# Cross attention and a gated mixture of projections: G/U slots moved by four places, loads and logits put earlier, ten weight pieces later

## Chip, core and metric

One core of one Trainium2 chip. The time is device time in microseconds (us) of one execution. PE is TensorE, DVE VectorE, ACT ScalarE, POOL GpSimd, SP SyncE, which here only issues DMAs.

## What is computed

64 batches of x (256 tokens x 256 channels), each with 77 context rows of 192 channels, all float32:

```python
def xattn(x, context):                     # 8 heads of 64
    q, k, v = heads(x @ Wq), heads(context @ Wk), heads(context @ Wv)
    return merge(softmax(q k^T / 8) v) @ Wo + bo
def ffn(h):                                # 16 experts
    rw = gating(h)      # softmax over the experts whose logit is positive (the top two if none is)
    q, k, v = [sum_e rw[:, e] * (h @ proj[e]) for proj in (q_proj, k_proj, v_proj)]
    attn = softmax(causal(q k^T / 8)) v
    return sum_e (attn * rw[:, e]) @ o_proj[e]
x = x + xattn(layernorm(x), ctx)
x = x + ffn(layernorm(x))
```

Gating's logits are `normalize(h) @ normalize(sim) - sigmoid(gates)`.

## The kernel before

**Products.** Every float32 operand is split into hi and lo parts (ACT writes hi, DVE subtracts to get lo), and `product` multiplies lo\*hi, hi\*lo and hi\*hi: lines 478, 479 and 480. Any product in the profile is in those lines, told apart by its tiles.

**Three phases, one step.** Phase a is cross attention of batch i+1, phase b the second layernorm, gating and expert projections of batch i, phase c the attention and output of batch i-1 (its last product, `c_y`, is of i-2). `step(i)` runs for i from -2 to 65, and each engine has its own hand-written order of the same step; semaphores join them. A step has an early half (slots E0 to E3, between scores of a and projections `b_qkv` 6 to 15) and a late half (M1, transpose XT, M2, `c_qk`, `b_qkv` 0, M3, `b_qkv` 1 and 2, `c_s`, the product Y with `uo`, `c_pT`, `b_qkv` 3, `c_pv`, `b_qkv` 4, L1, `b_qkv` 5, L2). I count position in a step from XT (line 537).

**G and U.** The context side is folded into the weights: for three batches (a group gm) 25 jobs make keys k0 to k3, values v0 to v3, G (k times Wq, g0 to g7) and U (v times Wo, u0 to u7), from the transposed context `ct`. The table `JOBS` puts them into the slots of three steps (i%3 = 0, 1, 2; I call these step 0, 1, 2). g0 to g7 and u0 to u7 go through one of two `draft` buffers (f%2) to DRAM (`store_g`, `store_u`), and come back per batch (`load_g` into `gq`, `load_u` into `uo`). `j_g(gm, f)` waits for k(f//2) to be taken out of PSUM, `j_u` for v(f//2). The jobs and phase a share three PSUM banks in the ring `A_ORDER`.

**Order of the loads.** SP issues in order and waits in order: behind a store that waits for DVE, every load waits too. `load_u(n)` needs all U of the group stored and Y of batch n-1 done; `load_x(n)` needs the sum xb of batch n-1 (POOL) and its layernorm.

**Gating chain.** `b_top` on DVE (logits z, line 1244, and top 8), `b_route_1` and `b_route_2` on POOL, `b_exp` on ACT, `b_wsum` on DVE, `b_rw` on POOL (line 1529). `b_first` on ACT (line 936) then scales `b_qkv` 0 and 1 by rw and frees their bank; PE needs that bank for `b_qkv` 3. `b_exp` stands on ACT behind `c_exp`, which needs `c_s` of DVE (line 1295).

**Opening.** Ahead of step -2 the group 0 is made in one go (`OPENING`), and the weights come in 16 pieces through three staging areas; pieces 6 to 13 are the expert projections (three DMAs each), 14 and 15 o_proj. `SPLIT_AFTER` puts pieces 6 to 10 into the opening, 11 to 15 are split in step -1.

Of the kernel before, what the change touches and what calls it, by code (L numbers as in the profile page):

```python
# [34 lines left out]
def xattn_moe_kernel(nc, x, ctx_in, Wq, Wk, Wv, Wo, bo, sim_matrix, gates, q_proj, k_proj, v_proj, o_proj, out, rw_dram):  # L35
# [67 lines left out]
    def job(i, slot):  # L103

        if slot not in JOBS[i % 3]:
            return None
        kind, f = JOBS[i % 3][slot]
        gm = i // 3 + (2 if kind == "ct" or i % 3 == 2 and kind != "u" else 1)
        return (gm, kind, f) if 1 <= gm < GROUPS else None
# [6 lines left out]
    with es:  # L116
# [219 lines left out]

        def loads_before(piece):
            return sum(len(PIECES[k][0]) for k in range(piece % SLOTS, piece + 1, SLOTS))
# [9 lines left out]
        def _(sp):  # L348
# [62 lines left out]
            def load_weights(pieces):  # L411
                for k in pieces:
                    if k >= SLOTS:
                        sp.wait_ge(wt_ready, k - SLOTS + 1)
                    for view, src in PIECES[k][0]:
                        sp.dma_start(view(stage[k % SLOTS]), src).then_inc(wt_in[k % SLOTS], 16)
# [7 lines left out]
            def step(i):  # L424
# [7 lines left out]

                if i % 3 == 2 and i // 3 + 3 < GROUPS:
# [4 lines left out]
                if i == -1:  # L438
                    load_weights((14,))
                if on(i + 2) and i + 2 > 0:  # L440
                    load_g(i + 2)
                if i == -1:
                    load_weights((15,))
# [6 lines left out]
                turn("E3")  # L450
                turn("M1")
                turn("M2")
# [6 lines left out]
            for hc, pieces in enumerate(((6,), (7, 8), (9,), (10, 11))):  # L459
                store_g(0, 2 * hc)  # L460
                store_g(0, 2 * hc + 1)
                load_weights(pieces)
            load_g(0)
            for hc, pieces in enumerate(((12,), (13,), (), ())):
                store_u(0, 2 * hc)
                store_u(0, 2 * hc + 1)
                load_weights(pieces)
# [7 lines left out]
        def _(pe):  # L475
# [257 lines left out]
            for k, (kind, f) in enumerate(OPENING):  # L733
                if k >= A_BANKS:
                    taken(0, *OPENING[k - A_BANKS])
                if kind == "ct":
                    j_ct(0)
                    query_weights()
                elif kind == "k":
                    j_k(0, f)  # L740
                elif kind == "v":
# [85 lines left out]
        def _(act):  # L827
# [6 lines left out]
            def split_weights(k):  # L834
                hi = PIECES[k][1]
                act.wait_ge(wt_in[k % SLOTS], 16 * loads_before(k))
                nc.scalar.activation(hi, stage[k % SLOTS][:, 0:hi.shape[1]], copy).then_inc(wt_hi, 1)
# [170 lines left out]
            for kind, f in OPENING:  # L1008
                if kind == "ct":
                    j_ct(0)  # L1010
                    query_weights()
                    ln1_b(0)
                elif kind == "k":
                    j_k(0, f)
                elif kind == "v":
# [8 lines left out]
            def step(i):  # L1024
# [22 lines left out]
                if i == -1:  # L1047
                    split_weights(11)
# [4 lines left out]
                if i == -1:  # L1053
                    split_weights(12)
                do(now, ln2_b)
                turn("E1")
                turn("E2")
# [4 lines left out]
                if i == -1:  # L1062
                    split_weights(13)
# [12 lines left out]
                if i == -1:  # L1076
                    split_weights(15)
# [10 lines left out]
                do(before, c_mix, 3)  # L1088
                turn("L2")

# [5 lines left out]
        def _(dve):  # L1096
# [11 lines left out]
            def split_weights(k):  # L1108
                dve.wait_ge(wt_hi, k + 1 if k < CC else k + 1 - CC)
                for lo, hi, rows, cols in PIECES[k][2]:  # L1110
                    last = V.tensor_tensor(lo, stage[k % SLOTS][rows, cols], hi.bitcast(F32), ALU.subtract)
# [212 lines left out]
            def step(i):  # L1324
# [23 lines left out]
                if i == -1:  # L1348
                    split_weights(11)
# [13 lines left out]
                do(now, b_norm, 2)  # L1363
                do(before, b_qkv, 11)
                if i == -1:
                    split_weights(12)
                turn("E1")
                do(earlier, c_y)
# [6 lines left out]
                if i == -1:  # L1375
                    split_weights(13)
# [13 lines left out]
                if i == -1:  # L1390
                    split_weights(15)
# [14 lines left out]
                do(now, b_qkv, 5)  # L1406
# [210 lines left out]
```

## Time and profile before

| | us |
|---|---|
| median of 3 runs | 2858.8 |
| lowest, highest | 2854.28, 2860.21 |
| the profiled execution | 2861.3 |
| its span | 2859.5 |
| PE busy in it | 2559.7 |
| DVE, ACT, POOL busy | 2158.7, 1581.5, 1105.5 |
| PE idle before Y (line 478, `uo`) | 83.3 in 21 waits |
| PE idle before `b_qkv` 3 | 73.0 in 43 waits |

Busy time of PE counts pipelined matmuls and is not PE at its peak. "<- issue" names no engine: the last semaphore came from something that the profile can't name, such as two DMAs counted by one semaphore.

### The profile page before, as it was taken

What the parts mean: (1) busy time and instruction counts of PE and PEld (TensorE: products, weight loads), DVE (VectorE), ACT (ScalarE), POOL (GpSimd) and SP (SyncE); (2) the same over time, 40 slices, a digit from 0 to 9 for tenths busy, and PEclk for the clock granted to TensorE, in tenths of its full rate; (3) what the DMA queues carried; (4) which work ended last, traced back from release to release, by engine and by line L of the source; (5) the groups of instructions that cost most, each with busy time, mean ns of one, the idle gap of its engine ahead of it and who ended that gap; (6) DMA issues with size and microseconds to landing.
All of it is one profiled execution on the core that took longest, in us unless ns stands there. A gap on an engine that the chain in (4) does not pass through costs nothing.

```text
span 2859.5 us, 54177 instructions
## 1 busy us (share of the span) xinstructions
PE 2559.7 (90%) x17308; PEld 2482.2 (87%) x17308; DVE 2158.7 (75%) x6107; ACT 1581.5 (55%) x5110; POOL 1105.5 (39%) x1739
## 2 busy tenths in 40 slices
PE   4599898999999898999899898999989899999987
PEld 3588898989889898989899898989889899989886
DVE  5477787877787787877777787877778787878774
ACT  4565565655555565555555565555555565556542
POOL 0134344434334344434334344434434434434442
PEclk6699999999999999999999999999999999999998
DMA  7555554454554554454555554454555455465531
GB/s 197 170 155 167 159 172 139 154 179 144 169 160 156 155 165 144 149 178 143 165 152 163 162 164 142 150 179 144 171 168 161 142 170 155 147 183 149 161 107 41
DMA packets 299938, 445.78 MB, mean 156 GB/s; under 512 B 36856, under 2 KB 210872, under 8 KB 291464
## 3 DMA queue, kind: packets, MB, share of 16 engines
q1 hardware_dynamic: 230024, 374.15, 41.2%
q10 hardware_dynamic: 69632, 68.17, 10.1%
q8 instruction: 140, 2.29, 0.4%
q14 instruction: 142, 1.16, 0.1%
HBM read 257.91 MB, written 184.35 MB: 155 GB/s over the span
## 4 chain that ended last, share of the span: by engine, by line
PE 62%; issue 11%; ACT 9%; POOL 7%; DVE 6%; ACTq 3%; DMA 2%; SPq 0%; POOLq 0%; DVEq 0%
PE bank_b L478 9%; PE bank_b L479 9%; PE bank_b L480 9%; PE bank_c L478 4%; PE bank_c L479 4%; PE bank_c L480 4%; PE bank_a L478 4%; PE bank_a L479 4%; PE bank_a L480 4%; ACTq L996 3%; POOL probs L1553 2%; PE bank_a L611 2%; PE bank_a L578 1%; DVE acc L1275 1%; DMA u_dram<-draft 1%
## 5 line engine op out<-in xcount | busy, mean ns | idle before, releaser
L478 PE MATMUL bank_b<-wqkv_hi,x2T_lo 128*128 128x384 f32 (+1 forms) x2048 | 732.1, 357 | 73.3 <-ACT acc L936 73.0
L1275 DVE SCALAR_TENSOR_TENSOR acc<-bank_b,rw,acc 128x192 f32<-128x192 f32 x1792 | 653.6, 410 | 93.5 <-PE bank_b L480 89.6
L479 PE MATMUL bank_b<-wqkv_lo,x2T_hi 128*128 128x384 f32 (+1 forms) x2048 | 698.0, 341 | 0.0
L480 PE MATMUL bank_b<-wqkv_hi,x2T_hi 128*128 128x384 f32 (+1 forms) x2048 | 695.0, 339 | 0.0
L1558 POOL TENSOR_TENSOR mixs_lo<-mix,mixs_hi 128x512 fp32r<-128x512 f32 x256 | 381.0, 1520 | 428.9 <-ACT mixs_hi L1005 428.9
L478 PEld LDWEIGHTS bank_b<-wqkv_hi,x2T_lo 128*128 128x128 f32 x2048 | 391.3, 191 | 85.2 <-ACT acc L936 83.4
L906 ACT ACTIVATE probs<-bank_a,s_max 128x77 f32<-128x77 f32 x1024 | 318.5, 327 | 259.3 <-DVE s_max L1208 259.0
L479 PEld LDWEIGHTS bank_b<-wqkv_lo,x2T_hi 128*128 128x128 f32 x2048 | 391.3, 191 | 0.0
L480 PEld LDWEIGHTS bank_b<-wqkv_hi,x2T_hi 128*128 128x128 f32 x2048 | 389.1, 190 | 0.0
L1553 POOL TENSOR_TENSOR probs<-probs,p_sum 128x616 f32<-128x616 f32 x128 | 156.6, 1223 | 393.7 <-DVE p_sum L1215 393.7
L1316 DVE TENSOR_TENSOR mix<-rw_all,late_tiles 128x512 f32<-128x512 f32 x256 | 281.1, 1138 | 24.5 <-ACT late_tiles L1001 24.5
L478 PE MATMUL bank_c<-wo_hi,mixs_lo 128*128 128x256 f32 x1024 | 287.6, 281 | 3.7 <-POOL mixs_lo L1558 3.7
L480 PE MATMUL bank_c<-wo_hi,mixs_hi 128*128 128x256 f32 x1024 | 286.8, 280 | 0.0
L479 PE MATMUL bank_c<-wo_lo,mixs_hi 128*128 128x256 f32 x1024 | 286.6, 280 | 0.0
L478 PE MATMUL bank_a<-uo,pT_lo 128*128 128x256 f32 (+1 forms) x640 | 203.1, 317 | 83.4 <-issue 83.3
L1005 ACT ACTIVATE mixs_hi<-mix 128x512 fp32r<-128x512 f32 x256 | 159.8, 632 | 158.8 <-DVE mix L1316 158.8
L1538 POOL TENSOR_TENSOR mix<-acc 128x192 f32<-128x192 f32 x128 | 76.3, 596 | 374.1 <-DVE acc L1275 373.0
L478 PEld LDWEIGHTS bank_a<-uo,pT_lo 128*128 128x128 f32 (+1 forms) x640 | 142.4, 223 | 87.4 <-issue 87.0
L906 ACT ACTIVATION_READ_ACCUMULATOR probs<-bank_a,s_max 128x1 f32 x1024 | 210.9, 206 | 0.0
L1181 DVE TENSOR_TENSOR both<-bank_a,only 64x231 fp32r<-64x231 f32 x352 | 138.9, 395 | 84.1 <-ACT both L865 81.7
L479 PE MATMUL bank_a<-uo,pT_hi 128*128 128x256 f32 (+1 forms) x640 | 199.4, 312 | 0.0
L480 PE MATMUL bank_a<-uo,pT_hi 128*128 128x256 f32 (+1 forms) x640 | 198.1, 309 | 0.0
(206 smaller groups left out, 6472.6 us busy)
## 6 DMA issues: line engine op xcount, KB each, us to landing
g_dram<-draft SPq DMA_DIRECT2D x176, 462.0 KB
gq<-g_dram SPq DMA_DIRECT2D x64, 1232.0 KB, 5.7
uo<-u_dram SPq DMA_DIRECT2D x64, 1024.0 KB
rw_all<-rw_dram ACTq DMA_DIRECT2D x128, 512.0 KB, 7.1
u_dram<-draft SPq DMA_DIRECT2D x176, 308.0 KB
xt<-in_x_dram SPq DMA_DIRECT2D x64, 256.0 KB, 4.2
out_dram<-mix SPq DMA_DIRECT2D x64, 256.0 KB, 6.3
u_dram<-draft SPq DMA_DIRECT2D x88, 156.0 KB
```

Source lines behind the costliest of these rows:

```text
L478: nc.tensor.matmul(dst, lhs[1], rhs[0], start=start, stop=False)
L479: nc.tensor.matmul(dst, lhs[0], rhs[1], start=False, stop=False)
L480: return nc.tensor.matmul(dst, lhs[0], rhs[0], start=False, stop=stop)
L906: last = nc.scalar.activation(probs[:, t, h * NC:(h + 1) * NC], bank_a(f"S{j}")[:, k * NC:(k + 1) * NC], ACT.Exp, bias=s_max[:, j, k:k + 1 ...
L996: nc.scalar.dma_start(rw_all[k * D:(k + 1) * D, :, :], rw_dram[:, :].rearrange("(a k) t -> k a t", k=2)[k].partition_broadcast(D)).then_in ...
L1005: nc.scalar.activation(mixs[0][:, 2 * j:2 * j + 2, :], mix[:, 2 * j:2 * j + 2, :], copy).then_inc(mix_hi, 1)
L1181: last = V.tensor_tensor(both[rows, k, e, cols], src[rows, cols], only.bitcast(F32)[rows, k, e, cols], ALU.subtract)
L1275: V.scalar_tensor_tensor(acc[:, t, k, :], src, rw[:, t, e:e + 1], acc[:, t, k, :], ALU.mult, ALU.add).then_inc(b_evac, 1)
L1316: V.tensor_tensor(mix[:, 2 * j:2 * j + 2, :], rw_all[:, 2 * j:2 * j + 2, :], aT2[:, :].unsqueeze(1).to_broadcast([P, 2, T]), ALU.mult).the ...
L1538: G.tensor_tensor(qkv[:, t, :], acc[:, t, 0, :], acc[:, t, 1, :], ALU.add).then_inc(qkv_ready, 1)
L1553: G.tensor_tensor(part, part, p_sum[:, half, 1, :, :].unsqueeze(3).to_broadcast([P, NT, HB, NC]), ALU.mult).then_inc(p_ready, 1)
L1558: G.tensor_tensor(mixs[1][:, 2 * j:2 * j + 2, :], mix[:, 2 * j:2 * j + 2, :], mixs[0].bitcast(F32)[:, 2 * j:2 * j + 2, :], ALU.subtract).t ...
```

## The change

1. `JOBS`: the jobs stand one to three slots earlier than before, k2 alone stays in L1 (g0 to g3 and k0 to k3 are now all in step 2, g4 opens step 0, and u6, u7 end step 1 instead of opening step 2). U of a new group is loaded at the head of step 2.
2. SP: `load_x(i+3)` at the end of step i instead of `load_x(i+2)` near its start; POOL: `a_xb(i+2)` at the end of step i instead of `a_xb(i+1)` between `c_mix` and `power` at its start.
3. DVE: `b_top` ahead of `c_qk`, `b_index` ahead of slot M2.
4. Opening: pieces 6 to 15 are split in steps -1, 0 and 1; `query_weights` runs behind k1; pieces get an explicit staging table.

```diff
-    JOBS = ({"E0": ("g", 3), "E1": ("k", 3), "E2": ("g", 4), "E3": ("g", 5), "M1": ("v", 0), "M2": ("g", 6), "L1": ("g", 7),
-             "L2": ("v", 1)},
-            {"E0": ("u", 0), "E1": ("u", 1), "E2": ("v", 2), "E3": ("u", 2), "M1": ("u", 3), "M2": ("v", 3), "M3": ("u", 4),
-             "L1": ("ct", 0), "L2": ("u", 5)},
-            {"E0": ("u", 6), "E1": ("u", 7), "E2": ("k", 0), "E3": ("k", 1), "M1": ("g", 0), "M2": ("g", 1), "L1": ("k", 2),
-             "L2": ("g", 2)})
+    JOBS = ({"E0": ("g", 4), "E1": ("g", 5), "E2": ("v", 0), "E3": ("g", 6), "M1": ("g", 7), "M2": ("u", 0), "L1": ("v", 1),
+             "L2": ("u", 1)},
+            {"E0": ("v", 2), "E1": ("u", 2), "E2": ("u", 3), "E3": ("v", 3), "M1": ("u", 4), "M2": ("u", 5), "M3": ("ct", 0),
+             "L1": ("u", 6), "L2": ("u", 7)},
+            {"E0": ("k", 0), "E1": ("g", 0), "E2": ("k", 1), "E3": ("g", 1), "M1": ("g", 2), "M2": ("g", 3), "L1": ("k", 2),
+             "L2": ("k", 3)})
...
+        STAGE = (0, 1, 2, 0, 1, 2, 0, 1, 2, 0, 1, 2, 1, 2, 1, 1)
...
-        SPLIT_AFTER = {("k", 1): (W_V,), ("k", 2): (W_O - 1, W_O), ("k", 3): (6,), ("v", 0): (7,), ("v", 1): (8,),
-                       ("u", 0): (9,), ("u", 2): (10,)}
+        SPLIT_AFTER = {("k", 1): (W_V,), ("k", 2): (W_O - 1, W_O)}
...
 # SP, step(i)
+                if i % 3 == 2 and on(i + 1) and i + 1 > 0:
+                    load_u(i + 1)
                 turn("E0")
-                if on(i + 2) and i + 2 > 0:
-                    load_x(i + 2)
...
                 turn("E1")
-                if i % 3 == 2 and on(i + 1) and i + 1 > 0:
-                    load_u(i + 1)
...
                 turn("M2")
-                turn("M3")
                 if i % 3 != 1 and on(i + 2):
                     load_u(i + 2)
+                if on(i + 3) and i + 3 > 0:
+                    load_x(i + 3)
                 turn("L1")
...
 # DVE, step(i)
                 do(nxt, a_xT)
+                do(now, b_top)
                 do(before, c_qk)
+                do(now, b_index)
                 turn("M2")
-                do(now, b_top)
-                do(now, b_index)
                 do(before, c_s)
...
 # POOL, step(i)
                 for j in range(4):
                     do(earlier, c_mix, j)
-                do(ahead, a_xb)
...
                 do(now, b_rw)
+                do(nxt, a_xb)
```

The weight pieces' loads and splits stand in the same way in the steps: 6, 7, 8 are loaded behind g7's store and split at E1, E2, M1 of step -1; 9 and 10 in L1 and L2 of step -1; 11 to 14 in step 0; 15 in step 1 (it was 11 to 15 in step -1).

SP around the head of a step 2, before (from the context loads to the step's U load and the output store; `draft` rows are stores of u6, then u7):

```order
L363 DMA ct<-in_ctx_dram 116x192
L364 DMA ct<-in_ctx_dram 116x64
L363 DMA ct<-in_ctx_dram 115x192
L364 DMA ct<-in_ctx_dram 115x64
L378 DMA u_dram<-draft 77x2x512
L378 DMA u_dram<-draft 39x2x512
L353 DMA xt<-in_x_dram 128x2x256
L388 DMA gq<-g_dram 128x2464
L378 DMA u_dram<-draft 38x2x512
L378 DMA u_dram<-draft 77x2x512
L397 DMA uo<-u_dram 128x4x512
L399 DMA uo<-u_dram 104x512
```

The same place now:

```order
L379 DMA u_dram<-draft 38x2x512
L379 DMA u_dram<-draft 77x2x512
L364 DMA ct<-in_ctx_dram 116x192
L365 DMA ct<-in_ctx_dram 116x64
L364 DMA ct<-in_ctx_dram 115x192
L365 DMA ct<-in_ctx_dram 115x64
L398 DMA uo<-u_dram 128x4x512
L400 DMA uo<-u_dram 104x512
L389 DMA gq<-g_dram 128x2464
```

The U load stands directly behind the context loads, u6 and u7 are stored before them, and x was loaded before this point.

DVE in the late half of a step 2, before (xT\_lo is behind XT, L1286 is `c_qk`, the draft is slot M2's, L1244 to L1257 are `b_top` and `b_index`, L1295 is `c_s`):

```order
L1167 TENSOR_TENSOR xT_lo<-bank_a,xT_hi 128x512
L1286 TENSOR_TENSOR mixs_hi<-bank_c,q_rows 64x256
L1286 TENSOR_TENSOR mixs_hi<-bank_c,mixs_hi 64x256
L1196 TENSOR_TENSOR draft<-bank_a,draft 128x2x3x77
L1244 SCALAR_TENSOR_TENSOR z<-bank_b,rn,sig 128x16 x2
L1249 MAX top<-z 128x8 x2
L1255 MAX_INDEX idx<-top,z 128x8 x2
L1257 CAST idxf<-idx 128x16
L1295 ISA mix,m<-bank_c,causal 128x128
```

And now:

```order
L1183 TENSOR_TENSOR xT_lo<-bank_a,xT_hi 128x512
L1260 SCALAR_TENSOR_TENSOR z<-bank_b,rn,sig 128x16 x2
L1265 MAX top<-z 128x8 x2
L1302 TENSOR_TENSOR mixs_hi<-bank_c,q_rows 64x256
L1302 TENSOR_TENSOR mixs_hi<-bank_c,mixs_hi 64x256
L1271 MAX_INDEX idx<-top,z 128x8 x2
L1273 CAST idxf<-idx 128x16
L1212 TENSOR_TENSOR draft<-bank_a,draft 128x2x3x77
L1311 ISA mix,m<-bank_c,causal 128x128
```

z and its maximum went ahead of `c_qk`, and the draft behind the index.

PE where step 2 meets step 0, now (the last row of k3 in slot L2, `b_qkv` 6, then g4 in E0, which needs k2 of slot L1):

```order
L561 MATMUL bank_a<-cT_hi,wk_hi 128x232
L482 MATMUL bank_b<-wqkv_hi,x2T_lo 128x384
L483 MATMUL bank_b<-wqkv_lo,x2T_hi 128x384
L484 MATMUL bank_b<-wqkv_hi,x2T_hi 128x384
L482 MATMUL bank_b<-wqkv_hi,x2T_lo 128x384
L483 MATMUL bank_b<-wqkv_lo,x2T_hi 128x384
L484 MATMUL bank_b<-wqkv_hi,x2T_hi 128x384
L582 MATMUL bank_a<-both,wq 128x232
```

Before, L2 held g2 and E0 held g3, which both need k1 of slot E3; k2 was first needed by g4 in E2 of step 0.

## Rows read from the trace of the kernel before

**Rows 1.** The page: span, busy time and share, granted clock in 40 slices

```profile
span 2859.5 us, 54177 instructions
PE 2559.7 (90%) x17308; PEld 2482.2 (87%) x17308; DVE 2158.7 (75%) x6107; ACT 1581.5 (55%) x5110; POOL 1105.5 (39%) x1739
PEclk6699999999999999999999999999999999999998
```

**Rows 2.** Waits of PE, whole span: total us, times, longest us

```profile
PE bank_a L478 <- issue: 83.3, 21, 4.9
PE bank_b L478 <- ACT acc L936: 73.0, 43, 2.0
PE bank_a L611 <- POOL probs L1553: 43.8, 21, 8.8
PE bank_a L578 <- DVE both L1181: 12.4, 22, 2.9
```

**Rows 3.** Timeline, PE and ACT, late half of step 32: start, us, [idle <-releaser]

```profile
1501.56 0.28 PE L680 MATMUL bank_c<-mixs_hi,q_rows 128*128 128x256 f32 x1
1505.02 0.55 PE L478 MATMUL bank_a<-uo,pT_lo 128*128 128x256 f32 x1 [3.18 <-issue]
1511.37 0.42 PE L478 MATMUL bank_b<-wqkv_hi,x2T_lo 128*128 128x384 f32 x1
1506.26 0.73 ACT L936 ACTIVATE acc<-bank_b,rw 128x192 f32<-128x192 f32 x2 [2.26 <-POOL rw L1529]
```

**Rows 4.** Timeline, SP: u5's store, x load, u7's store, U load

```profile
1472.97 0.64 SPq L378 DMA_DIRECT2D u_dram<-draft  x2
...
1480.66 0.51 SPq L353 DMA_DIRECT2D xt<-in_x_dram  x1
1489.07 0.66 SPq L378 DMA_DIRECT2D u_dram<-draft  x2
1496.54 0.38 SPq L397 DMA_DIRECT2D uo<-u_dram  x1
```

**Rows 5.** Timeline, DVE and POOL, early half of step 32

```profile
1486.17 0.75 DVE L1126 BATCH_NORM_STATS2 stats<-xt 128x6 f32<-128x256 f32 x2 [3.79 <-DMA xt<-in_x_dram]
1487.77 1.22 POOL L1553 TENSOR_TENSOR probs<-probs,p_sum 128x616 f32<-128x616 f32 x1 [5.42 <-DVE p_sum L1215]
```

**Rows 6.** Busy by stretch: length, engines, PEclk, DMA share, GB/s

```profile
1503.70:1510.50 6.80, 5.48 (x26) 5.51 (x27) 1.07 (x5) 1.03 (x5) 1.70 (x6) 0.50 0.35 118
1462.80:1466.20 3.40, 3.40 (x14) 3.40 (x13) 2.08 (x6) 0.85 (x3) 0.00 (x0) 0.50 0.12 44
52.00:82.00 30.00, 8.30 (x30) 6.25 (x29) 7.77 (x13) 6.95 (x16) 0.00 (x0) 0.50 0.65 189
```

**Rows 7.** Timeline, step 30, XT at 1410.66: `b_qkv` 1, then the gating chain

```profile
1413.93 0.34 PE L480 MATMUL bank_b<-wqkv_hi,x2T_hi 128*128 128x400 f32 x1
1415.86 0.37 DVE L1244 SCALAR_TENSOR_TENSOR z<-bank_b,rn,sig 128x16 f32<-128x16 f32 x2
1417.17 0.29 DVE L1295 CUSTOM_DVE_ANT_0 mix<-bank_c,causal 128x128 f32<-128x128 f32 x1
1418.40 0.21 ACT L926 ACTIVATE w<-g 128x32 f32<-128x32 f32 x1
1420.60 0.24 POOL L1529 TENSOR_TENSOR rw<-w,w_sum 128x32 f32<-128x32 f32 x1 [0.50 <-DVE w_sum L1263]
1421.66 0.44 PE L478 MATMUL bank_b<-wqkv_hi,x2T_lo 128*128 128x384 f32 x1 [1.67 <-ACT acc L936]
```

**Rows 8.** Timeline, PE and DVE, step 32 into 33: k2's evacuation and E0

```profile
1517.82 0.27 PE L578 MATMUL bank_a<-both,wq 128*128 128x232 f32 x1
1519.63 0.80 DVE L1181 TENSOR_TENSOR both<-bank_a,only 64x231 fp32r<-64x231 f32 x2 [0.36 <-ACT both L865]
```

**Rows 9.** Timeline, opening, DVE and PE

```profile
81.00 0.69 DVE L1203 TENSOR_TENSOR draft<-bank_a,draft 116x512 fp32r<-116x512 f32 x1 [3.97 <-ACT draft L899]
101.96 2.37 PE L611 MATMUL bank_a<-ident,probs 128*128 128x128 f32 x10 [8.79 <-POOL probs L1553]
```

More of the change, by code:

```diff
@@ L107, in job @@
         kind, f = JOBS[i % 3][slot]
-        gm = i // 3 + (2 if kind == "ct" or i % 3 == 2 and kind != "u" else 1)
+        gm = i // 3 + (2 if kind == "ct" or i % 3 == 2 else 1)
         return (gm, kind, f) if 1 <= gm < GROUPS else None
@@ L335, in xattn_moe_kernel @@
         assert len(PIECES) == W_O2 + 1 and all(piece[1] is None or piece[1].shape[1] <= SP_COLS for piece in PIECES)
+        STAGE = (0, 1, 2, 0, 1, 2, 0, 1, 2, 0, 1, 2, 1, 2, 1, 1)
         def loads_before(piece):
-            return sum(len(PIECES[k][0]) for k in range(piece % SLOTS, piece + 1, SLOTS))
-        SPLIT_AFTER = {("k", 1): (W_V,), ("k", 2): (W_O - 1, W_O), ("k", 3): (6,), ("v", 0): (7,), ("v", 1): (8,),
-                       ("u", 0): (9,), ("u", 2): (10,)}
+            return sum(len(PIECES[k][0]) for k in range(piece + 1) if STAGE[k] == STAGE[piece])
+        SPLIT_AFTER = {("k", 1): (W_V,), ("k", 2): (W_O - 1, W_O)}
         block = es.enter_context(nc.Block())
@@ L413, in load_weights @@
                     if k >= SLOTS:
-                        sp.wait_ge(wt_ready, k - SLOTS + 1)
+                        sp.wait_ge(wt_ready, max(p for p in range(k) if STAGE[p] == STAGE[k]) + 1)
                     for view, src in PIECES[k][0]:
-                        sp.dma_start(view(stage[k % SLOTS]), src).then_inc(wt_in[k % SLOTS], 16)
+                        sp.dma_start(view(stage[STAGE[k]]), src).then_inc(wt_in[STAGE[k]], 16)
             load_weights(range(0, 1))
@@ L450, in step @@
                 turn("E3")
+                weights(-1, 10)
                 turn("M1")
+                weights(-1, 11)
+                weights(0, 14)
                 turn("M2")
-                turn("M3")
                 if i % 3 != 1 and on(i + 2):
                     load_u(i + 2)
+                if on(i + 3) and i + 3 > 0:
+                    load_x(i + 3)
                 turn("L1")
                 turn("L2")
[L459 to L462, printed above, removed]
+            for f in range(H):
+                store_g(0, f)
             load_g(0)
[L464 to L467, printed above, removed]
+            load_weights(range(6, 9))
+            for f in range(H):
+                store_u(0, f)
             load_u(0)
@@ L737, in _ @@
                     j_ct(0)
-                    query_weights()
                 elif kind == "k":
                     j_k(0, f)
+                    if f == 1:
+                        query_weights()
                 elif kind == "v":
@@ L1010, in _ @@
                     j_ct(0)
-                    query_weights()
-                    ln1_b(0)
                 elif kind == "k":
                     j_k(0, f)
+                    if f == 1:
+                        query_weights()
+                        ln1_b(0)
                 elif kind == "v":
@@ L1110, in split_weights @@
                 for lo, hi, rows, cols in PIECES[k][2]:
-                    last = V.tensor_tensor(lo, stage[k % SLOTS][rows, cols], hi.bitcast(F32), ALU.subtract)
+                    last = V.tensor_tensor(lo, stage[STAGE[k]][rows, cols], hi.bitcast(F32), ALU.subtract)
                 last.then_inc(wt_ready, 1)
@@ L1406, in step @@
                 do(now, b_qkv, 5)
+                if i == -1:
+                    split_weights(9)
+                if i == 0:
+                    split_weights(14)
                 turn("L2")
+                if i == -1:
+                    split_weights(10)
             dve.wait_ge(small_in, 48)
@@ L1432, in _ @@
                     j_ct(0)
-                    query_weights()
                 elif kind == "k":
                     j_k(0, f)
+                    if f == 1:
+                        query_weights()
                 elif kind == "v":
```

63 lines of the change are left out of this document (40 added, 23 removed).

## The prediction

> **What bounds the kernel.** The page comes first: PE is busy 90% of the span, DVE 75%, and nothing else is near [rows 1]. So PE sets the time, and what can be won lies in three places: its idle time, the stretches at the lower clock, and the two ends. The matmuls themselves stay as they are. Next the waits of PE [rows 2]: 83.3 us before Y, 21 times and thus once in three steps; 73.0 us before `b_qkv` 3, 43 times, so in two steps of three; 43.8 us before the transposes of probs, 21 times. Third the timeline around one wait of each kind [rows 3, 5, 7], to see who is late and what PE loses in all. A loss counts here from where PE would have gone on, since the wait before Y has a longer shadow than its idle time: the granted clock was 0.50 over the stretch that holds it [rows 6], that is 1.2 GHz, where nearly every slice of the page has nine tenths or more of 2.4 [rows 1]. Groups of three steps repeat 21 times, so the sum is made for one group and multiplied. It is made against the profiled execution's 2861.3 us, 2.5 above the median of 2858.8.
>
> **U of a new group (step 2).** Before, u7 is stored at 1489.07 and the load is issued at 1496.54, when that store has landed; the first matmul that needs it starts at 1505.02 [rows 3, 4]. Store to load is 7.5 us and load to use 8.1 us (1505.02 less 1496.97, where its second DMA goes out). Now u7 is in slot L2 of step 1, where u5 was: stored at 1472.97 [rows 4]. The load can go at about 1472.97 + 7.5 = 1480.5 and is in at 1488.6 to 1489, some 13 us before PE asks at 1501.84 (the end of 1501.56 + 0.28, rows 3). Even if the steps shrink by 3 us it is hidden. The SP queue stands still for those 7.5 us behind u7; what queues behind it is the load of G, which waits for this step's last scores anyway, and g0's store.
> What that gives: Y and `c_pT` occupied PE from 1505.02 to 1511.37, mostly at half clock [rows 3, 6]. At full clock throughout the same 33 instructions take less, between 3.2 (half) and 6.35 us; I take 3.9, since the last part ran at full clock already. PE would be at `b_qkv` 3 at 1505.7 (it starts Y right behind `c_s`, at 1501.73), where the next wait is late: ACT frees the bank with the instruction of 1506.26 + 0.73 = 1507.0 [rows 3]. So the removed wait gives 1511.37 - 1507.05 = 4.3 us, and a gating wait of 1.3 us comes to light in step 2.
> The Trainium skill, page "TensorE: Matmul & The Clock Gate", section "HAM oscillation — how this bites in real kernels", says that a long DMA wait inside a matmul loop sends the array back to the slow clock, so that each next piece starts cold. By that rule, the trace agrees: the clock of the first row of rows 6. It would leave short waits free of charge. The second row of rows 6 speaks against that here: 0.50 right behind a gating wait of 1.72 us.
>
> **x earlier.** In step 2 the load of x stands behind the context loads and u6's store and goes out at 1480.66 [rows 4]; DVE waits 3.79 us for it, and p_sum, probs and the transposes follow [rows 5]. In the other steps x is in time. Now it is issued behind xb at the end of the step before, more than 20 us ahead, so this wait and PE's 43.8 us go. Of these 13.3 are the opening's (8.79 of them in one wait [rows 9]); 30.5 / 18 = 1.7 us per group. Next late there is PE itself. POOL's xb, 1.3 us, moves from a place where POOL waits for DVE later anyway to one where it has just written rw and is idle: nothing.
>
> **Logits ahead.** In step 30 z starts at 1415.86, 5.2 us behind XT, DVE having done `c_qk` and M2 first; z needs only `b_qkv` 1, which PE ends at 1413.93 + 0.34 = 1414.27 [rows 7]. So z can start 1.5 us sooner. What then sets rw? Not POOL's part but the two things that join it: `b_exp` at 1418.40 on ACT, which stands behind `c_exp` and so behind `c_s` at 1417.17, and on DVE `c_p` ahead of `b_wsum` [rows 7]. `c_s` hardly moves: `c_qk` now ends 0.4 us later (z and the maximum are ahead of it), PE's `c_s` follows by as much, and DVE gets there at about 1417.0. From there: `c_p` done 1419.1, `b_wsum` 1419.5, rw 1419.9, bank free 1420.7 instead of 1421.6. Gain 0.9 us, with PE's own 0.4 us at `c_s` already inside, since the bank is still last. Bounds: 0 (if M2's draft waits for the store of E3, which now uses the same draft buffer, and holds `c_s` back) and 1.67, the whole wait. I take 0.9 in steps 0 and 2. In step 1 slot M3 (now `ct`, 0.6 us on DVE) lies between `c_p` and `b_wsum`, so 0.3. Together 2.1 us per group.
>
> **G and U slots.** PE's work is the same. What matters is distance. k2 stays in L1, but g4, its first user, moves from E2 to E0, one projection and one job behind it. In step 32 PE is at E0 at 1517.82, and k2 is taken out at 1519.63 + 0.80 = 1520.43, because DVE reaches L1 only after the four mix products and ACT only after the third [rows 8]. PE must wait 2.6 us there, once in a group; those times hang on `c_pv` just ahead, so they move along with PE. Bounds: 0 if DVE gets there sooner, and 2.6 plus a fall of the clock behind every one (1.7 us: half of a 3.4 us stretch at 0.50 [rows 6]). Looking behind each wait, 9 of 42 gating waits (1.7 to 1.9 us) were followed by such a stretch, and all 21 waits for U; I take 0.4 for a wait between them in length, thus 0.7 us, and 3.3 us in all. By the skill's rule for long waits alone it would be 2.6, and the time 15 us lower.
> The other couplings have room: v1 in L1 is first needed in E1, k3 in L2 by g6 in E3, k0 in E0 by g0 in E1. The wait of M2 for the bank of E3 when that is a k or v (12.4 us in 22 [rows 2]) moves from step 2 to step 1. Two steps now have two k or v in the early half, each holding ACT for four copies and DVE in order behind them: I give 0.6 us a group, between 0 and 1.5.
> Fewer short waits also mean fewer slow stretches: 12 of them lie outside the waits for U, some 20 us in all or 1.0 a group; half of that, 0.5, goes.
>
> **Opening and end.** 26 to 82 us is a chain of draft buffers: ACT fills, DVE subtracts, SP stores, ACT waits for the landing. While the projections' pieces ran there, the DMA engines were busy 65% of 52 to 82 us [rows 6], and PE 8.3 of 30 us. Eight pieces of 384 KB leave. But the chain's last part is latency: an odd U store lands about 7 us after issue (7.5 above, in a steady step), and u1 to u7 is three such rounds. I give 3 us there and 3 more because x of batch 1 lands earlier than for the wait at 101.96 [rows 9]; behind k1 the later `query_weights` delays g0 by up to 4, and pieces 11 to 15 add ACT and DVE work of 0.8 to 1.2 us each to steps 0 and 1, mostly beside idle time. I keep 4 us gain, between 15 gain and 8 loss. The end is untouched.
> The skill's page "DMA: Bandwidth & Descriptors", section "Specifications", puts full rate at 512 B and more, and these pieces move in 256 B runs: by that, taking them out would free more than their bytes, and the gain would be nearer 15 us. No row here shows the price of a run.
>
> **Sum.** Per group: 4.3 (U) + 1.7 (x) + 2.1 (logits) + 0.5 (clock) - 3.3 (g4) - 0.6 (two k or v) = 4.7 us; times 21 = 99; with the opening 103. 2861.3 - 103 = 2758, less the 2.5 between profile and median: 2756.
>
> **Rivals.** (A) *g4 doesn't wait*, or under half a us: for it, that DVE's idle time before these mix products shrinks; against it, both ends hang on `c_pv`. Then 21 x 3.3 = 69 us less: 2687. (B) *The chain doesn't shorten*: the draft in M2 waits for E3's store (a G store beside the output's) and `c_s` comes later; 21 x 2.1 = 44 us more: 2800. Together with a clock that falls after every g4 wait (1.0 x 21 more): 2821. (C) *Slower*: U's load still ends last. If u7's store goes out over 13 us later than u5's did, because DVE's L2 or the x load ahead of it in the queue is late, the 4.3 us stay, and PE pays g4's wait on top: 4.7 - 4.3 - 0.9 (the gating wait in step 2 is hidden again) = -0.5 a group, 2859 + 10 - 4 = 2865. (D) *The table doesn't move what it says*: excluded by the order of the instructions.
>
> **Chances.** Forecast, within 2725 to 2785: 0.5. A, 2665 to 2725: 0.17. B, 2785 to 2830: 0.22. C: 0.05. Others, slower by something I don't see: 0.06. The range leaves out the ends of A and all of C: 2690 to 2825. A measurement of this kernel can tell about 0.2%, 6 us, from no change. Faster by more than that: 0.89; within: 0.04; slower: 0.07.
>
> **What would show it.** Right: no "issue" wait before Y and no 0.50 stretch in the middle of step 2; no DVE wait for x in steady steps; the waits before `b_qkv` 3 under 1 us in steps 0 and 2 and near 1.4 in step 1; a new group of some 21 waits of PE at line 582 for DVE's `both`, near 2.6 us each; three steps, XT to XT, shorter by 4.7 us. Wrong: waits for U that stay (C), or a new wait of the early half, for which DVE's order would be the reason.

## The result, and the profile after

| | before | after |
|---|---|---|
| median (runs) | 2859.5 (4) | 2787.9 (4) |
| profiled execution, its span | 2861.3, 2859.5 | 2798.0, 2796.2 |
| ratio, 95% interval | | 0.975 (0.971 to 0.979) |

Faster by 2.5%, 72 us; the forecast was 103. The four runs after lie between 2776.4 and 2798.0. In the profiled executions the difference is 63. The page after, against [rows 1]:

```profile
span 2796.2 us, 54177 instructions
PE 2540.1 (91%) x17308; PEld 2455.6 (88%) x17308; DVE 2163.7 (77%) x6107; ACT 1581.0 (57%) x5110; POOL 1102.6 (39%) x1739
```

Waits of PE, whole span (total us, times, longest us), against [rows 2]:

```profile
PE bank_c L683 <- DVE mixs_hi L1302: 66.2, 64, 4.6
PE bank_a L582 <- DVE both L1197: 50.8, 21, 2.5
PE bank_b L482 <- ACT acc L941: 37.0, 54, 1.4
...
PE bank_a L615 <- POOL probs L1580: 8.4, 3, 4.5
```

The wait before Y (83.3 us) is gone, that for probs is the opening's alone, that before `b_qkv` 3 is halved, and g4's wait is new (50.8 us in 21). All of this was forecast. L683 is `c_s`, which waits for `c_qk` of DVE, once a step. The forecast's term for the logits had 0.4 us of it in every step. Over 18 steady groups (batches 6 to 59) it is 0.45 in steps 0 and 1, as forecast, and 2.28 in step 2, which wasn't.

To see where time went, take the length from one XT to the next. Four starts on PE, of batches 36 to 39 (steps 1, 2, 0):

```profile
1546.38 0.60 PE L541 MATMUL bank_a<-ident,probs 128*128 128x128 f32 x4
1586.27 0.60 PE L541 MATMUL bank_a<-ident,probs 128*128 128x128 f32 x4
1632.57 0.60 PE L541 MATMUL bank_a<-ident,probs 128*128 128x128 f32 x4
1671.44 0.60 PE L541 MATMUL bank_a<-ident,probs 128*128 128x128 f32 x4
```

These are 39.9, 46.3 and 38.9 us; before, the same three took 43.5, 43.9 and 40.3. The mean over 18 steady groups, with the forecast's terms put where they belong:

| from XT of | before | after | moved by | forecast |
|---|---|---|---|---|
| step 1 | 42.91 | 40.29 | -2.62 | -1.7 (x) - 0.3 (logits) = -2.0 |
| step 2 | 44.59 | 45.65 | +1.06 | -4.3 (U) - 0.9 (logits) + 3.3 (g4) = -1.9 |
| step 0 | 40.42 | 38.88 | -1.54 | -0.9 (logits) |
| clock, anywhere | | | | -0.5 |
| two k or v, early halves of steps 1 and 2 (behind XT of steps 0 and 1) | | | | +0.6 |
| three steps | 127.93 | 124.81 | -3.12 | -4.7 |

The 18 groups give 56 of the 63 us; up to batch 6 the kernel is 3.7 us later than before, and from batch 60 to the end it gains 11.0. The gap to the forecast is in step 2, which grew although PE no longer waits for U there. SP ahead of XT at 1586.27 (starts of issues; `u_dram` x4 are u6's and u7's stores), against [rows 4]:

```profile
1565.64 2.16 SPq L379 DMA_DIRECT2D u_dram<-draft  x4
...
1577.16 0.39 SPq L398 DMA_DIRECT2D uo<-u_dram  x1
1577.59 0.47 SPq L400 DMA_DIRECT2D uo<-u_dram  x1
1578.17 0.35 SPq L389 DMA_DIRECT2D gq<-g_dram  x1
1579.09 0.38 SPq L370 DMA_DIRECT2D g_dram<-draft  x1
1579.95 0.38 SPq L405 DMA_DIRECT2D out_dram<-mix  x1
```

and ACT, then PE, behind it (L897 is the draft of g2 in M1, then of g3 in M2):

```profile
1591.29 0.56 ACT L897 ACTIVATE draft<-bank_a 128x462 fp32r<-128x462 f32 x1 [4.83 <-DMA g_dram<-draft]
1594.66 0.56 ACT L897 ACTIVATE draft<-bank_a 128x462 fp32r<-128x462 f32 x1 [0.89 <-DMA g_dram<-draft]
...
1594.80 0.30 PE L683 MATMUL bank_c<-mixs_hi 128*128 128x128 f32 x1 [3.76 <-DVE mixs_hi L1302]
```

Read it in this order. u7's store is issued by 1567.80, and U's load goes out at 1577.16, when that store has landed, 9.4 us on (the rows left out are four context loads, until 1573.3; then SP stands). Everything behind the wait goes out within 3.2 us: U (1.2 MB in two DMAs), G (1.2 MB), the store of g0, the output. The store of g0 goes out at 1579.09 and ACT is released by it at 1591.3, 12 us later. Over 18 steady groups the median from issue to landing of this store is 10.5 us (7.9 to 13.0), by the increments of its semaphore in the trace. ACT's draft of g2 writes the same draft buffer, and on ACT `c_qk` stands behind it, then `c_s` on PE. By the increments U had landed at 1584.7, G at 1589.2, the store at 1591.2. Two more loads were in flight beside them, those of `rw_all` (512 KB each), which ACT issues on its own queue at 1581.57 and 1582.21; they landed at 1591.5 and 1594.3. The DMA engines were busy 94% in that time (columns as in [rows 6]):

```profile
1577.10:1591.20 14.10, 13.88 (x97) 13.10 (x95) 8.92 (x26) 6.25 (x15) 4.41 (x7) 1.00 0.94 293
```

In all ACT waited 102.9 us for stores of G ahead of its drafts of G (7.9 before):

```profile
ACT draft L897 <- DMA g_dram<-draft: 102.9, 46, 5.7
```

The late `c_s` costs more than its wait: in the 18 steady groups 9 of its waits in step 2 are followed by a slow stretch. The one behind 1594.80:

```profile
1595.50:1598.90 3.40, 3.40 (x18) 3.40 (x18) 2.10 (x10) 1.27 (x6) 1.60 (x6) 0.50 0.42 144
```

The Trainium skill, page "DMA: Bandwidth & Descriptors", section "Queues, rings and completion order", says that an SDMA engine takes descriptors in ring order and that a semaphore's increment lands only after every earlier write of that engine. By that, a store behind two loads can't be counted before them; the landings above, in that order, agree.

### The profile page after: what moved, and what is told of

It reads as the page before. It is cut to its first block, busy times and chain, and to the rows that moved or that the text cites. A ratio compares the mean times of both kernels' runs of the same rounds, so it can differ in the third digit from the quotient of the medians.

```text
span 2796.2 us, 54177 instructions
## 1 busy us (share of the span) xinstructions
PE 2540.1 (91%) x17308; PEld 2455.6 (88%) x17308; DVE 2163.7 (77%) x6107; ACT 1581.0 (57%) x5110; POOL 1102.6 (39%) x1739
## 4 chain that ended last, share of the span: by engine, by line
PE 59%; DMA 14%; DVE 12%; ACT 7%; issue 5%; POOL 1%; SPq 1%; ACTq 0%; DVEq 0%; POOLq 0%
PE bank_b L482 9%; PE bank_b L483 9%; PE bank_b L484 9%; DMA u_dram<-draft 7%; DMA g_dram<-draft 7%; PE bank_c L482 5%; PE bank_c L483 4%; PE bank_c L484 4%; PE bank_a L482 3%; PE bank_a L483 3%; PE bank_a L484 3%; DVE acc L1291 3%; ACT mix L980 2%; PE bank_a L615 2%; DVE mix L1332 2%
## 5 line engine op out<-in xcount | busy, mean ns | idle before, releaser
L1508 POOL TENSOR_TENSOR pow_out<-pow_in,expo 128x2 f32<-128x2 f32 (+1 forms) x128 | 112.8, 881 | 306.4 <-DVE pow_in L1155 296.9
L482 PEld LDWEIGHTS bank_c<-wo_hi,mixs_lo 128*128 128x128 f32 x1024 | 196.6, 192 | 4.2 <-issue 3.8
L483 PEld LDWEIGHTS bank_c<-wo_lo,mixs_hi 128*128 128x128 f32 x1024 | 196.1, 192 | 0.0
L484 PEld LDWEIGHTS bank_c<-wo_hi,mixs_hi 128*128 128x128 f32 x1024 | 195.7, 191 | 0.0
L482 PE MATMUL bank_a<-uo,pT_lo 128*128 128x256 f32 (+1 forms) x640 | 186.7, 292 | 1.0 <-DVE xT_lo L1183 1.0
```

The costliest lines, as they stand in the source:

```text
L482: nc.tensor.matmul(dst, lhs[1], rhs[0], start=start, stop=False)
L483: nc.tensor.matmul(dst, lhs[0], rhs[1], start=False, stop=False)
L484: return nc.tensor.matmul(dst, lhs[0], rhs[0], start=False, stop=stop)
L1508: G.tensor_tensor(dst, src, expo[:, 0:m], ALU.pow).then_inc(ln_pow[k], 1)
```

## The experiments

Each kernel was timed beside the kernel before on the same chip. The ratio is against that; a difference between two kernels is the difference of their ratios, times 2859 for us. "Steps" are the means from XT of steps 1, 2 and 0.

| kernel | median | ratio (interval) | steps |
|---|---|---|---|
| changed, again | 2789.2 | 0.976 (0.974 to 0.978) | 40.21, 45.41, 38.93 |
| g0's store ahead of U and G | 2857.3 | 1.002 (1.001 to 1.003) | 40.17, 48.37, 38.91 |
| G behind g2's store | 2777.4 | 0.969 (0.966 to 0.971) | 40.14, 44.93, 38.93 |
| E0 behind S0 | 2767.7 | 0.971 (0.969 to 0.973) | 42.64, 40.19, 40.05 |
| E0 of step 0 later | 2727.2 | 0.952 (0.950 to 0.954) | 40.09, 42.19, 38.96 |
| opening of before | 2775.6 | 0.974 (0.972 to 0.977) | 40.09, 44.49, 38.88 |
| logits back | 2914.1 | 1.017 (1.013 to 1.021) | 42.20, 47.35, 40.16 |
| x back | 2906.1 | 1.014 (1.012 to 1.017) | 49.05, 41.61, 38.91 |
| before + slots, U | 2989.9 | 1.045 (1.041 to 1.049) | 50.86, 43.24, 40.56 |
| before + logits | 2819.0 | 0.986 (0.983 to 0.988) | 42.35, 44.31, 39.21 |
| before + x | 2797.6 | 0.980 (0.978 to 0.983) | 40.51, 43.70, 40.24 |
| put together | 2671.9 | 0.934 (0.932 to 0.936) | 40.19, 39.94, 38.92 |

**The changed kernel again.** 

> The changed kernel once more, as the measure for the runs beside it. 2788 within 12 us, and a spread of its own executions of more than 10 us (the kernel before: under 8), because how long the DMA store of g0 takes to land differs from group to group.

2789.2, from 2778.6 to 2794.3; the range of its own runs is 16 us, that of the kernel before 12 us in 17 runs, so the spread tells little.

**Is it the store's place in the queue?** In step 2:

```diff
 # cut; conditions on i left out
-                load_u(i + 1)      # head of step 2
-                load_g(i + 2)      # behind E0
                 turn("E1")         # store of g0
+                load_u(i + 1)
+                load_g(i + 2)
```

> The changed kernel; in step 2 the store of g0 (slot E1) is issued ahead of the loads of U and G instead of behind them. Theory (burst): the store takes 12 us to land because 2 MB of loads go into the same queue just ahead of it, and ACT's draft in M1, which writes the same draft buffer, waits for that landing and holds c_qk and c_s. Then the store lands within 6 us, ACT's wait at M1 is gone in step 2, PE's wait before c_s falls from 3.8 to under 1 us, step 2 (XT to XT) falls from 45.7 to about 43.5, the median to about 2743 (2730 to 2765), and the spread of the executions halves. Rival (work, not landing): step 2 is longer because two k and two g lie in its early half, and the draft waits only since it is early; then c_s comes no sooner, and the median stays at 2788 within 8 us.

g0's store did what the theory says, and the kernel became 2.6% slower than the changed one. SP, ACT and PE around XT at 1616.78 (L900 at 1616.98 is g2's draft in M1, without a wait; the next is g3's in M2):

```profile
1609.57 0.39 SPq L370 DMA_DIRECT2D g_dram<-draft  x1
...
1611.58 0.36 SPq L389 DMA_DIRECT2D gq<-g_dram  x1
...
1617.41 1.57 SPq L370 DMA_DIRECT2D g_dram<-draft  x2
...
1616.98 0.56 ACT L900 ACTIVATE draft<-bank_a 128x462 fp32r<-128x462 f32 x1
1626.70 0.56 ACT L900 ACTIVATE draft<-bank_a 128x462 fp32r<-128x462 f32 x1 [6.75 <-DMA g_dram<-draft]
```

U and G go out 6.7 and 5.2 us ahead of XT, where it was 9.1 and 8.1, so the burst lies 2 to 3 us nearer to XT and hits the next two stores: g1's goes out at 1617.41, ACT's draft of g3, which needs that buffer, is released 9.3 us later, and `c_exp` stands behind it in M2. Over the steady groups g0's store now lands 3.6 us after issue (median; 10.5 in the changed kernel), g1's 9.1 and g2's 9.9 (6.5 and 3.6 there). The mechanism holds (a store pays for what is in flight when it is issued); the expected 2743 is a miss, since I had thought of one store of three.

**G out of the way.** In step 2:

```diff
-                load_g(i + 2)      # behind E0
 ...
                 turn("M1")
+                load_g(i + 2)
```

> The changed kernel; in step 2 the load of G for the batch after next goes out behind the store of g2 (slot M1), 5 us behind XT, and no longer ahead of g0's store; U's load stays where the change put it. Theory (burst, after a_store_first, where g0's store landed 3.6 us after issue and the delay went to g1's and g2's, 9.1 and 9.9 us): with G out of the way of all three, each lands within 5 us of its issue or before its draft is due, ACT waits in neither M1 nor M2 of step 2, PE's wait before c_s is 0.45 us there as in the other steps, step 2 falls from 45.4 to about 43.2, the median to 2789 - 2.1 x 21 = 2745 (2735 to 2760). G is in at some 16 us behind XT and asked for at 23. Rival 1 (U's load alone is enough of a burst): g0's store still lands after XT, ACT waits 1 us or more in M1, and half is won, 2767. Rival 2 (G becomes the late one): the load meets U's of the next batch and x's, PE waits before the first scores of step 0, and the median is 2789 or more.

0.7%, 21 us less than the changed kernel, half of what was expected and the first rival's size, though mostly not its place. Over the steady groups ACT's wait in M1 of step 2 fell from 59.2 us in 18 to 12.3 in 11, and `c_s` waits 0.5 us; but the wait in M2, for g1's store, grew from 25.9 us to 54.3. That store lands 6.2 us after issue (median), hardly sooner than in the changed kernel (6.5). G's load goes out only 1.7 us behind it, so it wasn't out of this store's way. ACT's waits for G's stores, whole span:

```profile
ACT draft L899 <- DMA g_dram<-draft: 82.7, 34, 4.2
```

**The wait of g4.** First moved in all steps, and only in step 0 then:

```diff
 # cut. PE; ACT and DVE alike. First kernel, all steps (E0 stands behind S0 in A_ORDER too):
-                turn("E0")
                 do(before, c_rT)
                 do(before, b_qkv, 7)
                 do(earlier, c_y, 0)
                 fill("S0", ahead, a_s, 0)
+                turn("E0")
 # Second kernel, i % 3 == 0 alone: behind c_y 0, ahead of S0
```

> The changed kernel; slot E0 moved behind the first scores S0 on PE, ACT and DVE. PE then has c_rT, projection 7, a part of the output product and S0 ahead of g4, over 3 us of work that doesn't need k2. Theory (the wait costs what it lasts and the clock behind it): 21 waits of 2.5 us and the slow stretches behind some 12 of them (1.7 us each) leave, 53 + 20 = 73 us, less what ACT and DVE lose by E0's later place; about 2725 (2712 to 2745). Rival (the wait only absorbs): ACT and DVE are late by as much anyway, and PE meets them before the transposes of probs or before projection 3; then no more than a third is won, 2765 to 2788.

> The changed kernel; in step 0 alone the job of E0, g4, goes out behind c_rT, projection 7 and a quarter of the output product, which don't need k2, on PE, ACT and DVE alike; the scores stay behind it and steps 1 and 2 are untouched. In the run with E0 behind S0 step 2 (which holds this place) fell by 5.2 us, while steps 0 and 1 grew by 1.1 and 2.4 since their own E0 was moved too. Theory: the wait of 2.5 us falls by the 1.8 us of work put ahead, the slow stretch behind it goes, 2.6 us a group, and steps 0 and 1 don't grow: 2789 - 55 = 2734 (2720 to 2750). Rival (the fall by 5.2 hangs on the scores ahead of g4, or on k0's later place in step 2, not on this wait): 2789 - 1.8 x 21 = 2751 at best, with slow stretches left, up to 2770.

With E0 behind S0 step 2 lost 5.2 us, but steps 1 and 0 grew by 2.4 and 1.1, and nothing had moved there but E0. PE waited 21.0 us in 27 for probs, 10.8 of it behind the 18 steady XT of step 0; that explains a part, and the rest stays open. So 0.5% was left, near the rival's figures. In step 0 alone the gain is 2.4%, 69 us, all behind XT of step 2 (-3.2, of which 2.4 is the wait and the rest the clock: 47.8 us at 0.50 in the 18 steady steps 2, against 78.5), and neither other step grew. PE has 2.6 us of other work, and g4 comes 0.2 us after k2 is out (1565.41 + 0.81 on DVE):

```profile
1563.72 0.38 PE L701 MATMUL bank_c<-ident,rw 128*16 128x128 f32 x2
...
1566.41 0.30 PE L582 MATMUL bank_a<-both,wq 128*128 128x232 f32 x1
...
1565.41 0.81 DVE L1203 TENSOR_TENSOR both<-bank_a,only 64x231 fp32r<-64x231 f32 x2 [0.36 <-ACT both L873]
```

**The opening.** The opening and the weight pieces of the kernel before, all else as changed (cut):

```diff
-            load_weights(range(6, 9))          # between G's and U's stores
+            # 6 to 13 between the stores, 14 and 15 in step -1, as before
-        STAGE = (0, 1, 2, 0, 1, 2, 0, 1, 2, 0, 1, 2, 1, 2, 1, 1)
+        # piece k in stage k % 3
```

> The changed kernel with the opening, the weight pieces and their stages as in the kernel before; slots, U, x and logits as changed. Theory: the first XT comes at 81.7 us again instead of 87.3 and batch 4's XT 4 to 7 us sooner, steady steps alike: 2788 - 6 = 2782 (2776 to 2787). Rival: what the opening lost comes back in steps 0 and 1, where pieces 11 to 15 are now split, or the changed opening is faster once x comes early: 2790 to 2800.

The median is 13.6 us lower; the intervals of the ratios overlap (0.976 and 0.974), but the trace is plain: batch 4's XT comes at 204.6 instead of 214.2. The changed opening costs some 10 us. Step 2 is 0.9 us shorter as well, which isn't the opening's doing: nothing differs there, but 7 of 18 waits of g4 were followed by a slow stretch, not 14. Of the eight pieces that the prediction lets leave the opening three stay, right in front of the U phase. SP and ACT after (L904: the draft of u2):

```profile
56.28 2.49 SPq L417 DMA_DIRECT2D mix<-in_L_ffn_k_proj_dram  x1
...
61.08 26.84 SPq L379 DMA_DIRECT2D u_dram<-draft  x16
...
65.79 0.60 ACT L904 ACTIVATE draft<-bank_a 116x512 fp32r<-116x512 f32 x1 [10.41 <-DMA u_dram<-draft]
```

**Logits and x taken back,** each alone, on the changed kernel:

```diff
 # DVE
-                do(now, b_top)
                 do(before, c_qk)
-                do(now, b_index)
                 turn("M2")
+                do(now, b_top)
+                do(now, b_index)
 # the other kernel, SP (and a_xb on POOL back as well)
                 turn("E0")
+                load_x(i + 2)
 ...
-                load_x(i + 3)
```

> The changed kernel with the maximum of the logits and its index back behind the routed queries and M2 on DVE. Prediction's theory: rw comes 0.9 us later in steps 0 and 2 and 0.3 in step 1, so PE waits that much more before projection 3: +2.1 a group, 2789 + 44 = 2833. Theory after the trace of the changed kernel: only step 0 got its 0.9, in steps 1 and 2 the drafts' waits for DMA hold c_s back and c_s, not the logits, sets rw; and c_qk comes 0.5 us sooner without the maximum ahead of it: +10 to +20, 2799 to 2809. Rival: within 5 us of 2789, the order is worth nothing.

> The changed kernel with the load of x and POOL's xb back at their places before. Theory: x in step 2 is late again by 3.8 us for DVE and the transposes of probs wait once a group; in the changed kernel context loads, U's, G's and the store of g0 stand in the queue at that place, so x may be later than before the change: +1.7 x 18 + 10 in the opening = 2830 (2820 to 2850). Rival: x's 0.5 MB no longer in the queue at step 2's M2, or U's load ahead of it, change what else is late: 2789 to 2815.

Each costs far more than its term: 4.1% (116 us) and 3.8% (109 us). With the logits behind M2, they stand behind the draft that waits for a landing: step 2 +1.9, step 1 +2.0, step 0 +1.2. With x at its old place it stands behind U's load, which waits for u7 (SP and DVE in step 1):

```profile
1633.14 0.39 SPq L398 DMA_DIRECT2D uo<-u_dram  x1
...
1634.13 0.39 SPq L354 DMA_DIRECT2D xt<-in_x_dram  x1
...
1640.80 0.75 DVE L1142 BATCH_NORM_STATS2 stats<-xt 128x6 f32<-128x256 f32 x2 [8.90 <-DMA xt<-in_x_dram]
```

8.9 us instead of 3.8 [rows 5], and step 1 is 8.8 us longer. Step 2 is 3.8 us shorter there: the delay gives the stores time to land (g0's 2.8 us after issue). ACT's draft in M1 waits 0.5 us there, and `c_s` 0.45. The clock differs too: 3.4 us of the 18 steady steps 2 were at 0.50, against 81.9 in the changed kernel, and one wait of g4 was followed by a slow stretch, not 12. So 41.61 is what step 2 takes when hardly a draft waits and the clock stays up.

**One part on the kernel before,** each alone: the new `JOBS` with `load_u(i + 1)` at the head of step 2; the DVE order; `load_x` and `a_xb`. The edits are those of the change:

```diff
 # first kernel
-            {"E0": ("u", 6), "E1": ("u", 7), "E2": ("k", 0), ...
+            {"E0": ("k", 0), "E1": ("g", 0), "E2": ("k", 1), ...
 # second kernel
+                do(now, b_top)
                 do(before, c_qk)
 # third kernel
-                    load_x(i + 2)
+                    load_x(i + 3)
```

> The kernel before with the slots and U's load as changed; x, logits and opening stay as before. The prediction's terms: 4.3 (U) - 3.3 (g4) - 0.6 (two k or v) = 0.4 a group, 2859 - 8 = 2851. Theory after the runs that took x and logits back (they cost 5.3 and 5.0 us a group there, not 1.7 and 2.1): the table alone puts x behind a queue that stands 10 us for u7's landing, and the logits behind drafts that wait for landings; 2789 - 14 + 110 + 110 = 2995 (2950 to 3020), that is 5% slower than before, by waits of PE before the transposes of probs in step 1 (9 us a group) and before projection 3. Rival (the two share a wait, each is hidden in the other's): 2880 to 2920.

> The kernel before with the logits' maximum and index ahead of the routed queries and M2 on DVE, nothing else. The prediction's theory: the wait before projection 3 falls from 1.7 to 0.8 us, c_s being next: 0.9 in steps 0 and 1 and nothing behind U's wait in step 2: 2859 - 1.8 x 21 = 2821 (half clocks left out 5 to 10 more). Rival (in the kernel before no draft of M2 waits long, so the order is worth less than in the changed kernel, since c_s comes 0.4 later and rw with it): within 10 us of 2859.

> The kernel before with the load of x a step earlier and POOL's xb behind rw, nothing else. In the changed kernel taking this back cost 109 us. The prediction's theory: on the kernel before it is worth the wait for x alone, PE's 30.5 us in 18 steady groups, 1.7 a group or 36, and up to 10 in the opening: 2859 - 40 = 2819 (2810 to 2828); the 5.2 us a group of the changed kernel then come from the load of U that stands ahead of x in the queue there. Rival (x early is worth as much by itself, because DVE's statistics move and give time everywhere): 2859 - 109 = 2750. Rival 2 (with the slots of before the probs wait only hides the next one, PE at the stores of u7 or k0): above 2835.

The slots and U's load alone make the kernel 4.5% slower (2990 measured, 2995 expected from the runs before, 2851 by the prediction's terms). PE waits before the transposes of probs, and before `b_qkv` 3 more than before the change:

```profile
PE bank_a L611 <- POOL probs L1553: 128.1, 23, 7.5
PE bank_b L478 <- ACT acc L936: 103.1, 64, 2.2
```

The logits alone bring 1.45%, 41 us, the forecast's 44. Of the wait before `b_qkv` 3, 26.5 us are left of 73.0, and `c_s` waits instead:

```profile
PE bank_a L478 <- issue: 69.9, 21, 4.2
...
PE bank_c L679 <- DVE mixs_hi L1286: 31.1, 64, 2.6
PE bank_b L478 <- ACT acc L936: 26.5, 38, 1.1
```

x alone brings 2.0%, 56 us, more than the 40 expected and half of what the rival had.

**Put together.** The changed kernel, with the opening of before, E0 of step 0 later, and in step 2:

```diff
                 turn("E0")
-                load_g(i + 2)
 ...
                 turn("M2")
+                load_g(i + 2)
```

> The changed kernel with three things put right: the opening of the kernel before; in step 0 g4 behind c_rT, projection 7 and a quarter of the output product; in step 2 the load of G behind the store of g3 (slot M2), 8 us behind XT. Theory (burst and early use are all that step 2 still loses): without G in the queue the stores of g1 and g2 land in 3.3 us as those of g5 and g7 do in step 0, ACT waits in neither M1 nor M2 of step 2, c_s of DVE is at 6.4 us, rw at 9.0 to 9.2, step 2 falls from 45.4 to 38.9 as step 0: 2789 - 14 - 6.5 x 21 = 2639 (2635 to 2670). Rival 1 (G late): G is asked for at 17 us behind XT, is issued at 8 and shares the queue with U's and x's loads behind it; if it lands after 17, PE waits before the scores and half of the gain over a_e0_step0 goes: 2680 to 2710. Rival 2 (U's load alone still delays g0's store past M1, 0 to 3 us by group): 2670 to 2700.

2671.9, 6.6% faster than before and 4.2% faster than the change; mean granted clock 0.990 in the profiled execution (0.953 before, 0.966 after; a part of this is the opening, and the five executions, equally fast, have 0.979 to 0.991). Step 2 fell to 39.9, not to 38.9. ACT in it (g2's and g3's draft, XT at 1512.47):

```profile
1513.16 0.56 ACT L897 ACTIVATE draft<-bank_a 128x462 fp32r<-128x462 f32 x1 [0.49 <-DMA g_dram<-draft]
1518.97 0.56 ACT L897 ACTIVATE draft<-bank_a 128x462 fp32r<-128x462 f32 x1 [3.31 <-DMA g_dram<-draft]
```

So the stores still land late without G. For g0's store that is the second rival, U's load ahead of it. For g1's store, which holds M2, it is less direct. SP, then ACT:

```profile
1503.84 0.39 SPq L397 DMA_DIRECT2D uo<-u_dram  x1
...
1506.12 0.40 SPq L404 DMA_DIRECT2D out_dram<-mix  x1
1513.11 7.49 SPq L369 DMA_DIRECT2D g_dram<-draft  x3
```

```profile
1507.75 0.61 ACTq L1001 DMA_DIRECT2D rw_all<-rw_dram  x1
1508.39 1.02 ACTq L1001 DMA_DIRECT2D rw_all<-rw_dram  x1
```

g1's store is the first of the three, at 1513.11. By the increments U had landed at 1511.0 and the output's store at 1513.8; the loads of `rw_all` landed at 1515.5 and 1517.7, and g1's store at 1518.9, 5.8 us after issue. So U and the output are hardly beside it any more; 1 MB from another queue is. In each of the 19 groups between 300 and 2550 us the store landed 1.0 to 2.5 us behind the second of these loads, which go out 5.4 and 4.7 us ahead of it. How late they land goes with U: in five groups U's load went out 11 us or more ahead of g1's store, the second load of `rw_all` was in 2.0 to 3.2 us after the store's issue, and the store after 3.3 to 4.4; in 12 groups U had under 10 us, and it was 3.9 to 4.8 and 5.3 to 7.0. This points to U's load by way of `rw_all`; no run moved either alone, so it isn't shown.

## Why the prediction was right, and where it was off

The sign, the range and most mechanisms held; the size was 103 against 72. Point by point:

- **U, 4.3 us a group: the mechanism right, one price missing.** The wait is gone (from u7's store to U's load it takes 10.2 us, not 7.5, and there was room for it). What failed is the sentence on the SP queue: it names what queues behind u7, the load of G and g0's store, and gives them no price. They have one: they go out with U in one burst, and g0's store lands 10.5 us after issue. Step 2 took 45.65 us; it takes 41.61 where hardly a draft waits ("x back"). Of the difference, 4.0 us a group, some 1.0 is the clock behind g4's wait (11 slow stretches more in 18 groups, at the prediction's 1.7 us; an estimate). The other 3.0, 63 us over 21 groups, are the waiting drafts. PE's own rows give nearly as much: 1.8 more before `c_s`, 0.1 before `b_qkv` 3, and 0.85 for the nine slow stretches behind `c_s`. The draft that waits for a store's landing stood in the forecast as rival B, at E3 and M2 and with 2.1 us; it came at M1 as well and cost more. Without the 3.0 step 2 would have fallen by 1.9 us, which is the forecast, so its other terms hold as a sum; they weren't told apart.
- **g4, 3.3 us: right.** 50.8 / 21 = 2.4 us a group against 2.6, and taking it away gave 3.2 a group. The clock fell within 1 us of the end of 11 of the 21, and 1.2 and 1.4 us behind two more (0.5 to 0.6; I had 0.4). One of them:

```profile
738.70:742.10 3.40, 3.01 (x12) 2.92 (x13) 2.89 (x8) 2.19 (x6) 1.43 (x2) 0.50 0.05 13
```

  The Trainium skill, page "TensorE: Matmul & The Clock Gate", section "HAM oscillation — how this bites in real kernels", shows long DMA waits between the pieces of a matmul loop that send the array back to the slow clock. A rule for long DMA waits alone, as the prediction read it, would have left these 2.47 us waits for DVE without a slow stretch; the trace doesn't agree. In the prediction's own count one gating wait is missing (10 were followed by such a stretch, not 9), and one of the 21 waits for U was not followed by one (3.2 us, before 2399.6); the sum doesn't change by it.
- **x, 1.7 us: too small.** Alone on the kernel before it gives 3.5 (2.4 behind XT of step 1; 0.9 in step 2, where PE's wait for U is 0.6 shorter; 0.2 in step 0). I had counted PE's idle time and nothing that follows from it.
- **Clock, 0.5 us: not seen as such.** In the 18 steady groups 81.9 us were at 0.50, against 133.1 before. Of the 22 stretches 12 are behind g4's wait and nine behind `c_s`; the second had no place in the forecast.
- **Logits, 2.1 us: right.** The wait before `b_qkv` 3 fell from 1.69 to 0.25 us in step 0 and from 1.72 to 1.10 in step 1; less the 0.45 before `c_s` that is 1.0 and 0.2 (forecast 0.9 and 0.3). In step 2 it was 1.46 with the slots alone and 0.18 in "x back", a gain of 0.8 once the 0.45 is taken off (forecast 0.9). Taking it back costs 5.3 us a group, since there the logits stand behind the waiting drafts.
- **Opening, 4 us gain: wrong sign.** x early gives about 5 (batch 4's XT at 206.0 instead of 210.8), the moved pieces cost about 10. The step that failed is "eight pieces leave": three of the eight stay, and the U stores wait behind them on SP (10.41 us of ACT in one wait).
- **The sum.** The parts taken alone are +129 (slots, U), -41, -56 and +6 to +14, together some 40 us slower than before (the last by the ratios or by the medians). Measured is 72 faster. The 110 us between are not an error of one term: x and the logits cure what the slots do. My price for the slots was one for an order in which x and logits stand well already. That the sum came out in the range is in part luck: behind XT of steps 1 and 0 the kernel gained 4.2 us a group where 2.3 to 2.8 were forecast, and the waiting drafts took 3.0 that no term had.

## What to carry to other kernels

Where a load must wait for a store, look at everything that is issued behind it on that queue: it goes out as a burst, and the next store in the burst lands late, with whoever writes that buffer next. Look at the other engines' queues too: here ACT's loads were in flight at the same time. Price parts of a change in the order in which they cover each other, and test each alone. A wait of 2.5 us on PE may be removed by 2.6 us of work already there, in that one step only.

## What the runs showed of the hardware

A G store (462 KB) lands 10.5 us after issue (median of 18; 7.9 to 13.0) behind two loads of 1.2 MB each, and 9.1 us where it is issued 6 us behind G's load and the output's store; in both the two loads of `rw_all` on ACT's queue are in flight too. With these beside it and U's load already in it is 5.6 us ("put together", g1). In step 0, where no load of U precedes them, the four stores land 2.8, 2.9, 3.2 and 3.3 us after issue. During the burst the DMA engines were 94% busy at 293 GB/s, with a mean of 159 GB/s over the span. The granted clock fell to 0.50 within 1 us of the end of 11 of 19 waits of 2.47 us that were otherwise alike, and behind 10 of some 40 waits of 1.7 to 2.0 us before the change; what tells them apart stays open.
